# A megakernel of two attentions and two gated feed-forwards on one Trainium2 core: the inner layers of the first feed-forward by 7 products of quarters in place of 8

## The reference, cut to what matters

```python
x = L0_attn_x                                   # 4 batches, 1024 tokens, 256 wide, fp32
x = x + attention(layernorm(x))                 # 8 heads of 64 over a latent of 64
x = x + L0_ffn(layernorm(x))
x = x + attention(layernorm(x))                 # 16 heads of 16, rotary positions
x = x + gated_ffn(layernorm(x))                 # hidden 768, integer weights

def L0_ffn(x, w1_w, w1_s, w2_w, w2_s, h1_w, h1_s, h2_w, h2_s, w3_w, w3_s):
    h = silu(lin(x, w1_w, w1_s)) * lin(x, w2_w, w2_s)        # 256 -> 1024, twice
    h = gelu(lin(h, h1_w, h1_s))                             # 1024 -> 1024
    h = gelu(lin(h, h2_w, h2_s))                             # 1024 -> 1024
    return lin(h, w3_w, w3_s)                                # 1024 -> 256
# lin(x, w, s) = (x @ w.T) * s; the weights w are -1, 0 or 1, the scales s fp32
```

## Time and profile before

| | |
|---|---|
| runs | 2337.16, 2341.58, 2336.05 us |
| profiled execution | 2332.85 us, its span 2331.0 us |
| granted clock, mean | 0.996 |
| TensorE busy | 2286.6 us, 98% |
| ScalarE busy | 1463.2 us, 63% |
| VectorE busy | 1378.5 us, 59% |
| GpSimd busy | 1001.8 us, 43% |
| first attention | 0 to 722.6 us |
| first feed-forward | 722.6 to 1460.4 us |
| second attention | 1460.4 to about 2182 us |
| last feed-forward | to 2331 us |

### The profile page before, as it was taken

How to read it: one execution, slowest core, us unless ns; L and a number is a source line. 1 busy time by engine, 2 the same in 40 slices (tenths; PEclk the granted TensorE clock), 3 DMA queues, 4 the chain that set the end, 5 groups by cost and what they waited for, 6 DMA issues and landing times.

```text
span 2331.0 us, 39372 instructions
## 1 busy us (share of the span) xinstructions
PE 2286.6 (98%) x14921; PEld 1414.8 (61%) x14921; DVE 1378.5 (59%) x2150; ACT 1463.2 (63%) x2049; POOL 1001.8 (43%) x646
## 2 busy tenths in 40 slices
PE   7999999999998999999999999999999999999999
PEld 5455555555556888888888886444444444444688
DVE  6655766666743143232232224889889889998364
ACT  5777777777764444444444443678777777778643
POOL 2676766757763373664655645120100000000354
PEclk9999999999999999999999999999999999999999
DMA  2213222222214455555555546343332332331232
GB/s 63 69 52 100 82 74 84 82 80 76 74 31 165 158 178 183 183 182 192 182 175 190 193 165 190 92 105 77 90 87 59 93 82 64 92 90 41 81 112 77
DMA packets 156841, 259.07 MB, mean 111 GB/s; under 512 B 37004, under 2 KB 97292, under 8 KB 156300
## 3 DMA queue, kind: packets, MB, share of 16 engines
q1 hardware_dynamic: 156652, 256.53, 36.6%
HBM read 206.52 MB, written 60.68 MB: 115 GB/s over the span
## 4 chain that ended last, share of the span: by engine, by line
PE 63%; ACT 2%; DVE 1%; issue 1%; DMA 1%; SPq 1%; POOL 0%; POOLq 0%
PE m_R L130 47%; PE m_O L130 11%; PE m_X L130 4%; ACT m_P L1813 1%; DMA m_K<-bounce_k 1%; PE m_X L227 1%; SPq L1671 0%; DVE m_mraw L1965 0%; ACT m_OS L1820 0%; PE m_X L2179 0%; DVE m_ln_x L206 0%; PE m_R L227 0%; DMA inverses<-m_rinv 0%; DVE m_ln_stat L184 0%; SPq L1698 0%
## 5 line engine op out<-in xcount | busy, mean ns | idle before, releaser
L1965 DVE TENSOR_REDUCE m_mraw<-m_R 128x2 f32<-128x1024 f32 x512 | 622.6, 1221 | 68.5 <-PE m_R L130 56.0
L1813 ACT ACTIVATE m_P<-m_R 128x1024 f32<-128x1024 f32 x512 | 523.7, 1025 | 148.6 <-PE m_R L130 148.3
L130 PE MATMUL m_O<-m_P,m_V 128*17 128x256 f32 x4096 | 329.4, 393 | 4.4 <-ACT m_P L1813 2.5
L785 DVE CUSTOM_DVE_ANT_0 a_excess<-a_X,a_excess 128x512 f32<-128x512 f32 x256 | 166.5, 688 | 170.6 <-PE a_X L130 167.9
L955 POOL TENSOR_TENSOR a_accp<-a_accp,a_P 128x1024 f32<-128x1024 f32 x96 | 253.9, 2645 | 24.5 <-ACT a_P L631 16.2
L631 ACT ACTIVATE a_P<-a_S 128x1024 f32<-128x1024 f32 x256 | 249.7, 1040 | 8.5 <-PE a_S L130 8.5
L2070 POOL TENSOR_TENSOR m_act0l<-m_xf,m_act0h 128x512 fp32r<-128x512 f32 x128 | 164.8, 1290 | 209.2 <-ACT m_xf L1875 110.9
L130 PE MATMUL m_R<-m_act0h,wt 128*128 128x512 f32 x640 | 251.4, 393 | 0.0
L130 PE MATMUL m_R<-m_act0l,wt 128*128 128x512 f32 x640 | 250.4, 391 | 0.0
L130 PE MATMUL a_O<-a_P,a_V 128*64 128x512 f32 x1024 | 247.7, 605 | 0.0
L130 PE MATMUL m_R<-m_Q,m_K 64*128 64x512 f32 x800 | 200.1, 497 | 2.3 <-DVE m_mraw L1965 2.0
(11 more groups left out here) (274 smaller groups left out, 4130.1 us busy)
## 6 DMA issues: line engine op xcount, KB each, us to landing
wt<-wcopy SPq DMA_DIRECT2D x176, 512.0 KB, 3.3
m_K<-bounce_k SPq DMA_DIRECT2D x96, 128.0 KB, 5.5
m_ln_x<-x SPq DMA_DIRECT2D x23, 512.0 KB, 4.0
a_tile<-in_L_ffn_tiles SPq DMA_DIRECT2D x22, 512.0 KB, 3.6
wcopy<-in_L_ffn_tiles SPq DMA_DIRECT2D x22, 512.0 KB, 5.0
x<-xres SPq DMA_DIRECT2D x78, 128.0 KB, 1.7
m_Q<-bounce_q SPq DMA_DIRECT2D x150, 64.0 KB, 2.3
xres<-x SPq DMA_DIRECT2D x64, 128.0 KB, 2.7
```

The source lines that it names most:

```text
L130: return pe.eng.matmul(out, lhsT, rhs, start=start, stop=stop, skip_group_check=True)
L785: dve.eng.tensor_tensor_reduce(excess[:, h, :], bank(key), excess[:, h, :], 1.0, LOWEST, ALU.add, ALU.max, mraw[u % 2][:, q, h:h + 1]).the ...
L1813: act.eng.activation(P[h % 4][:, :, :], pair(key)[:, :, :], ACT.Exp, scale=SCALE).then_inc(R.free(key))
L1965: dve.eng.tensor_reduce(mraw[u % 2][:, at, :], pair(key)[:, :, :], AX.X, ALU.max).then_inc(R.free(key))
```

## The change

For a batch's two blocks at once, weights W and activations X are cut in quarters (two halves of the features; two blocks), and W X is made with 7 products of quarters and sums of quarters (the variant of Strassen and Winograd).

- The feed-forward runs by batch: 640 products in 128 slots, 5 to a slot. Gate and up of both blocks are 128, each inner layer 224 (m1, m2, m6, m7, m4, m5, m3, 32 each), down 64. START stays 512.
- m1 and m2 add into the same banks, and so do m5 and m3; ScalarE keeps a copy of m1 (`keep_first`), which m2's matmul waits for.
- A *leave* on VectorE adds a bank to what is kept (m6, m7, m4, m5, m3). Gelu then runs in place in SBUF on ScalarE (`gelu`), for m2 from the bank.
- A *mix* on VectorE makes the four sums t3, t1, t2, t4 of activation quarters, four dependent operations with both sources in SBUF, for each of four tiles j.
- Every operand gets its high part on ScalarE (`high`) and its low part on VectorE or GpSimd (`by_pool`).
- A batch has 40 weight tiles. Four sums of quarters per layer and half (16 tiles) are made in the first attention on VectorE and stored behind the copies in `wcopy`; the compares come every 3 turns for it, and write int8 on the way.
- Side work of blocks 6 and 7 runs in the second attention, c by c; projections of the even block begin at slot 32 of a batch's first half, those of the odd one at 26 of its second.
- The first 24 maxima come every second slot from START - 56 on and use one pair of banks; the Y ring has the other four then.
- The rest of `ffn_attention_ffn` follows: buffers shared with the attention's, fills moved, query tiles fetched earlier.

```diff
@@ first attention @@
-    LOWS0, LOWS, LOW_FIRST = 22, 27, 6
+    LOWS0, LOWS, LOW_FIRST = 22, 27, 4
+    MIXES, MIX_STEPS = 4, 8
+    MIX_FIRST = LOW_FIRST + 3 * LOWS0
+    LAST_FIRST = MIX_FIRST + MIXES * MIX_STEPS + 1
...
+            def mix_moves(n, step):
+
+                if step == 0:
+                    sp.wait_ge(s_low, LOWS0)
+                    if n:
+                        store_mix(n - 1, 2)
+                    if n < MIXES:
+                        load_quarter(n, 1, 1, 1)
+                        sp.wait_ge(s_mixed, 64 * n)
+                        load_quarter(n, 0, 1, 0)
+                elif step == 2:
+                    store_mix(n, 0)
+                    load_quarter(n, 1, 0, 0)
+                elif step == 4:
+                    store_mix(n, 1)
+                    load_quarter(n, 1, 0, 1)
+                elif step == 6:
+                    store_mix(n, 3)
+                    load_quarter(n, 1, 0, 0)
+                    sp.wait_ge(s_mixed, 64 * n + 48)
+                    load_quarter(n, 0, 1, 0)
...
+            def mix(n, step):
+
+                first, second = tile[:, :], f32(tile_hi[:, :])
+                dve.wait_ge(s_quarter[0], 16 * (2 * n + (1 if step < 7 else 2)))
+                dve.wait_ge(s_quarter[1], 16 * (4 * n + (step + 1) // 2))
+                if step == 1:
+                    dve.eng.tensor_tensor(first, first, second, ALU.add).then_inc(s_mix)
...
+                if mix_at(u, j) and mix_at(u, j)[1] % 2:
+                    mix(*mix_at(u, j))
@@ the other three stages @@
-    NB, MT, PER, SLOTS = 8, HID0 // 128, 22, 64
-    WFREE = NB * PER
+    NB, MT, PER, SLOTS, PACE = 8, HID0 // 128, 40, 64, 5
+    WFREE = B * PER
...
+    FIRST_MAX = START - 2 * ML - 8
...
-    BACK = (2, 4, 6, 8)
-    C_LOAD, C_STATS, C_SCALE, C_TURN = 10, 15, 18, (22, 24)
...
+    BACK = (6, 8, 10, 12, 14, 16, 18, 20)
+    C_LOAD, C_STATS, C_SCALE, C_TURN = (16, 10), (21, 15), (24, 18), ((28, 30), (22, 24))
...
+        if FIRST_MAX <= H < FIRST_MAX + 2 * ML:
+            return (H - FIRST_MAX) // 2 if (H - FIRST_MAX) % 2 == 0 else None
...
-        k, s = divmod(H, SLOTS)
-        return (k, 11 * s // 2, 11 * (s + 1) // 2) if k < NB else (k, 0, 0)
...
+        s, at = divmod(H, 2 * SLOTS)
+        return (s, PACE * at, PACE * at + PACE) if s < B else (s, 0, 0)
...
+    for l in range(2 * B):
+        for j in range(4):
+            if l % 2:
+                H = (640 * (l // 2) + 128 + 192 + 8 * j + 7) // PACE + 2
+            else:
+                H = high_slot(("b22", l, j)) + 2
+            mixes.setdefault(H, []).append((l, j))
...
+            def keep_first(key):
+
+                _, l, m = key
+                act.wait_ge(*done(key))
...
+            def leave(key):
+
+                name, l, m = key
+                bank = psY[Y.slot(bank_of(key))][:, :]
+                dve.wait_ge(*done(key))
+                if name == "m6":
...
+                    dve.eng.tensor_tensor(twos[m], bank, kept[m], ALU.add).then_inc(Y.free(key))
...
+            def mix(l, j):
+
+                x11, x12, x21, x22 = [whole[place][j] for place in ("11", "12", "21", "22")]
+                n = 4 * mix_order[l, j]
+                dve.wait_ge(*(gelu_done(l - 1, "12", j) if l % 2 else up_done(l, "12", j)))
+                dve.wait_ge(*low_done(("b22", l, j)))
+                dve.eng.tensor_tensor(x22, x22, x12, ALU.subtract).then_inc(s_mixed)
+                dve.wait_ge(s_mixed, n + 1)
+                dve.wait_ge(*low_done(("b11", l, j)))
+                dve.eng.tensor_tensor(x12, x12, x11, ALU.subtract).then_inc(s_mixed)
+                dve.wait_ge(s_mixed, n + 2)
+                dve.eng.tensor_tensor(x11, x22, x11, ALU.add).then_inc(s_mixed)
+                dve.wait_ge(s_mixed, n + 3)
+                dve.wait_ge(*low_done(("b21", l, j)))
+                dve.eng.tensor_tensor(x21, x21, x11, ALU.subtract).then_inc(s_mixed)
...
+                    elif key[0] in ("m6", "m7", "m4", "m5", "m3"):
+                        leave(key)
+                for op in lows_at(H, False):
+                    low(op)
+                for l, j in mixes_at(H):
+                    mix(l, j)
...
+                if H == START - 10:
+                    for i in range(5):
+                        fill_late(i)
...
+                    if key[0] == "m2":
+                        pe.wait_ge(s_kept, 4 * key[1] + key[2] + 1)
```

553 lines of the change are left out of this document (391 added, 162 removed).

## The result

The kernel after takes 2441.96 us (median of four runs, 2440.67 to 2454.36), the kernel before beside it 2337.75 (four, 2336.05 to 2341.58): a ratio of 1.0455, 95% interval 1.0419 to 1.0491. It is slower, by 104 us where 14 were forecast, and lies 64 us above the end of the range. One of e8's four runs took 9928.2 us at a granted clock of 0.195, and is left out of its numbers.

A forecast was written before the change was run, and what follows sets the result against it. TensorE was taken to bound the first feed-forward, with VectorE almost as full in the second attention. Products saved 58.1 us, added waits and costs outweighed them: +14.4 on 2337.2 gave 2351.6, say 2352 us (range 2312 to 2378).

The forecast's parts named there:

- First attention: VectorE waits for weight quarters fetched behind the inverses: 3 us for each of mixes 1 to 3, 9 (0 to 15).
- The compares: First attention: compares every 3 turns instead of 4 cost nothing, hidden in VectorE's idle time; otherwise 2 us each.
- Clock: TensorE's granted clock drops after long waits, 1.7 us lost after one gap; 3.4 us in all (0 to 6.8).
- Place 1: Slots 21 to 32, batches 1 to 3: TensorE waits while mixes meet c's normalisation; 30.0 us (22 to 37).
- Products: First feed-forward: 256 fewer products at 0.227 us each, 58.1 us less on TensorE's path.
- Collisions: VectorE slowed beside GpSimd when using SBUF: 0.77 us each, 2.5 us (0 to 5) per Place 1.
- Place 2: Slots 67 to 80, odd layer's mixes: third m2 waits for ScalarE's c11 copy; batches 0 to 2, 10.8 us (4 to 17).
- Batch 3's tail: Batch 3's odd-layer mixes with the first 24 maxima: TensorE waits 9.0 plus 3 us (whole tail 5 to 18).
- Sending: Slots 90 to 106: SP waits for GpSimd when sending projections, weight loads behind; 2 us (0 to 8).
- Block 6 in the second attention: Block 6's side work takes 15.0 us there against 10.7 in the feed-forward: moving it costs 4.3 us.
- The seam: GpSimd's late fills and the first exponentials at the start of the second attention: 1 us (0 to 5).
- everything at its upper bound: Rival, slower still: all listed waits at their upper bounds, +55, 2392 us at most; 2372 to 2390 has chance 0.10.

The follow-up runs named there:

- e8: Kernel after with mix fetches first, residual and V fetches moved, t2's parts, even c normalisation and projection sends later, projections wider apart; 2385.81 us, ratio 1.0203.
- e2: Kernel after with the first attention's weight-quarter sums working on only 16 of 1024 columns; first attention 784.0 us, whole span 2433.0.
- e3: Kernel after with SP storing sums and fetching the next quarters at the start of a turn, not its end; first attention 733.3 us, whole span 2383.4.
- e1: Kernel after without the first attention's sums of weight quarters, their tiles filled by plain copies; first attention 730.8 us, whole run 2393.39.
- e12: Kernel after with the low parts of b22, t2 and t3 all on VectorE; first feed-forward 730.9 us, whole span 2425.6.
- e13: e9 with the low parts of b22, t2 and t3 all on VectorE; first feed-forward 725.2 us, whole span 2355.3.
- e5: Kernel after with the first backs' residuals loaded 12 half steps before the second attention and V fetched 12 before its batch; second attention 744.0 us, span 2427.2.
- e4: Kernel after with even halves' c normalisation, turns, projections and values 12 slots later; first feed-forward 740.2 us, whole span 2442.2.
- e14: e13 with even halves' c normalisation put ahead of the mixes and projections from slot 40; 2356.02 us, ratio 1.0072.
- e15: e14 with values 3 slots behind each projection instead of 2, and turns of c and b one to two slots later; 2343.41 us, ratio 1.0026.
- e10: Kernel after with GpSimd's low parts of first feed-forward operands replaced by zero fills; first feed-forward 706.1 us, whole span 2396.6.
- e9: e8 with c normalisation clear of the mixes in both halves, second attention's places as in the kernel after; 2366.8 us, ratio 1.0131.

## Why the prediction was wrong

The direction was right, the size was not: +14.4 forecast, +108.9 between the profiled executions. By stage the forecast was +9, -10.6 and +16; it became +72.1, +5.7 and +31.5, so that in the first feed-forward, which the change is about, even the direction was wrong.

- **First attention, 9 us forecast, 72.1 measured: the step that failed.** The mechanism was the one named (a quarter fetched behind the sending of the inverses). But the text let "a mix's first step" alone stand there, "3 us for each of mixes 1 to 3". A mix has 8 steps and a unit 4 turns, so step 4 meets j = 2 just as step 0 does, and also mix 0's: eight late quarters at 5.4 to 7.7 us of VectorE's time, 48.7 in all, not three of 4 to 5; TensorE waited 41.7 us behind them. The upper bound, 15, had the same gap. And no low clock was charged to a stage whose TensorE would stand for some 5 us once in a unit: 27.4 us more were lost to it than before. e2 (the sums nearly gone, the stage still 784.0) and e3 (the fetches moved, 733.3) show it. The compares, put at nothing, may not have been free: without the mixes (e1) the stage stays 8.2 us over the one before, with them and no late quarter (e3) 10.7. Which of the stage's other changes costs this was not tried.
- **Clock, 3.4 us (0 to 6.8): 55 measured.** The price came from one gap. In the kernel after, the two windows of 10 us with place 1's waits (2.8 and 4.9 us idle) have 0.83 and 0.66, which is 5.1 us lost behind 7.7 of waiting. 27 us of the 55 are in the first attention and went with its waits (e3).
- **Products, 58.1 us: right.** 0.227 us each, and 669.7 us plus the added idle (55.4) and clock time (20.5) gives 745.6, against 744.2 measured.
- **Place 1, 30.0 us (22 to 37): right in place and kind.** The waits are 7.7, 7.2 and 8.1 us, 23.1 in all; with the clock behind them (13.6) it is 36.7. The turns of slots 28 and 30 wait as worked out, with two whole mixes before L250; the third wait, at slot 32, did not come.
- **Collisions: single ones dearer than priced, the sum about right.** 0.77 us each was the price; in the mixes single operations lost 0.96 (1.65 against 0.69), and in e8 four scalings 2.9 (4.26 against 1.38). The sum holds 15.9 us for them (three times 2.5 and 2.3, and 1.5). At place 1 as shown above they cost VectorE 2.6 us, against 2.5: the two operations of 1.65 and 1.63 us, and one of 1.42 at 985.30. In all the mixes they cost it 21 us, and e12 and e13 got 13 and 17 us of time back by keeping them apart. By the rule that the prediction took from the Trainium skill (SBUF — State Buffer, "SBUF: two separate sides"), the engine that starts first holds the lock for its whole instruction. The trace agrees: the two long operations ended 0.55 and 0.54 us behind the end of GpSimd's beside them, and what they lost, 0.96 and 0.94 us, is less than GpSimd's whole 1.59 and 1.71.
- **Place 2, 10.8 us (4 to 17): right.** ScalarE's copy of the third c11 (the bank that m1 and m2 share) cost 2.97 us three times, and 2.2 in the first batch's even layer, which was not named: 11.1.
- **Batch 3's tail, 12 us (5 to 18): right within its bounds.** 1.5, 2.3, 0.7 and 1.5 us of waits, 6.0, and 3.5 of clock. But the first two are TensorE waiting for the leaves L2317, not for a maximum.
- **Sending, 2 us (0 to 8): 9.3,** the five waits called issue. They are weight tiles in SP's queue behind a send, which waits for GpSimd's low part (12.9 us of SP's time in 20).
- **The waits of the first feed-forward together, 54.8 us: 55.4 of added idle time.** That this fits so well is luck: place 1 and the tail came 13 us lower than forecast, sending 7 higher, and 6 us are in small waits on no list. What turned the stage's -10.6 into +5.7 is the clock, 20.5 us in it.
- **Block 6 in the second attention, 15.0 us: 17.5.** The seam, 1 us (0 to 5): 7.2, since the residual of the first back was loaded behind V's fetch, which waited for GpSimd's fills. The fetches of V moved to half step - 8: not forecast at all, 6.6 at the changes of batch. e5 gives back 6.5 of the first and 3.5 of the second; the later runs confirm the first only, so what makes K late stays open.

The rival "everything at its upper bound" ended at 2392, because it added the same list of places; the first attention's second late step was on no list. That the side work could be moved out of its places at no cost (e4, e8) was wrong as well: the idle time of VectorE and GpSimd could be used only in some places of the batch, and those were found with e14 and e15.

## What to carry to other kernels

When a periodic task (8 steps) is laid over a periodic queue (4 turns), list every step that meets the queue's slow turn, and give each of them the whole delay. Fetches that take no engine's time cost 61 us here by their place behind one wait in a DMA queue, and putting them at the front of the turn cost nothing. Where the work of TensorE shrinks and the work of two other engines grows, price the waits with the lower clock that they leave behind, and give two engines that slow one another down separate stretches of time before any fine placing.

## What was not expected of the hardware

- A fill on GpSimd (526 ns, nothing read) in place of its low part (1.3 us, two sources in SBUF) left every operation of the mixes at 682 to 693 ns (e10).
- The clock does not answer every wait alike, nor equal waits alike. A single wait of 2.97 us left its windows of 10 us at 1.00 (the one that ended at 896.07) or at 0.85 (at 1071.34), both for ScalarE's copy in the kernel after; one of 2.66 us left 1.00 (at 1128), and two of 2.8 and 5.0 us some 8 us apart left 0.83 and 0.66.
- The fetch of K at a change of batch varied between executions of the same code: unit 8 of the second attention (counted from 0) took 25.5, 29.6 and 28.7 us in the kernel after, in e1 and in e3. In e9, e13, e14 and e15, which share another version of that stage, it took 24.9, 30.2, 29.0 and 30.6. What sets that is open.
